# W_down of two tiles by seven block products, with the sums on GpSimd and VectorE

## The reference, cut to what matters

```python
# x: (8, 2048, 256); D = 256, INNER = 1024, 4 heads, 64 x 64 keys cut to 1024 experts
x = x + layernorm(attention(layernorm(x)))     # causal linear attention, and a memory
def ffn(hidden):
    ...                                        # scores of the keys, the best 8 of each head
    w = silu(einsum('btd,bthkd->bthk', hidden, de) * softmax(scores))
    experts_states = einsum('bthk,bthkd->btd', w, ue)
    dense = einsum('bti,di->btd', silu(einsum('btd,id->bti', hidden, W_up)), W_down)
    return dense + experts_states
x = x + layernorm(ffn(x))
```

## Time and profile before

| | us |
|---|---|
| median of 3 runs (lowest to highest) | 2823.78 (2823.51 to 2824.08) |
| the profiled execution | 2823.89 |
| its span, first to last instruction | 2822.1 |
| TensorE busy | 2796.8 |
| ACT busy | 2524.6 |
| DVE busy | 2425.9 |
| POOL busy | 2059.2 |

### The profile page before, as it was taken

One profiled execution on the slowest core, in us unless ns is written; L12 is line 12 of the kernel. 1 busy time (PEld: TensorE's weight loads), 2 busy tenths in 40 slices (PEclk: granted clock), 3 DMA queues, 4 the chain that ended last, 5 costly groups with the idle time before them and its releaser, 6 DMA issues.

```text
span 2822.1 us, 43258 instructions
## 1 busy us (share of the span) xinstructions
PE 2796.8 (99%) x11986; PEld 2179.2 (77%) x11986; DVE 2425.9 (86%) x6126; ACT 2524.6 (89%) x3619; POOL 2059.2 (73%) x2461
## 2 busy tenths in 40 slices
PE   8899999999999999999999999999999999999999
PEld 7677777777777777777777777777777777777777
DVE  6888888888888888888888888888888888888885
ACT  6888999999999899989999999999999999999997
POOL 4676777677777777777777777777777777777674
PEclk9999999999999999999999999999999999999999
DMA  4787888788878887887888888788877887887764
GB/s 131 153 172 165 173 171 173 165 176 175 170 164 176 173 167 168 174 174 165 174 173 170 165 176 175 168 164 178 174 166 169 175 173 166 173 171 167 150 152 116
DMA packets 609013, 471.27 MB, mean 167 GB/s; under 512 B 362371, under 2 KB 543492, under 8 KB 608772
## 3 DMA queue, kind: packets, MB, share of 16 engines
q0 software_dynamic: 52832, 199.77, 39.8%
q1 hardware_dynamic: 555940, 268.74, 38.3%
HBM read 137.37 MB, written 131.20 MB: 95 GB/s over the span
## 4 chain that ended last, share of the span: by engine, by line
PE 89%; POOL 5%; issue 2%; ACT 2%; DVE 2%; POOLq 0%; DVEq 0%; ACTq 0%
PE banks L763 83%; PE banks L945 4%; POOL sums L600 3%; PE banks L927 2%; POOL rstd L586 1%; POOL wexp L662 1%; ACT L1135 0%; POOL cand_best L645 0%; ACT wexp L1135 0%; DVE prob L1283 0%; DVE picked L1225 0%; POOL cdif L665 0%; DVE w_blocks L1298 0%; POOL cprob L614 0%; ACT scores L1152 0%
## 5 line engine op out<-in xcount | busy, mean ns | idle before, releaser
L600 POOL TENSOR_TENSOR sums<-scores 128x1024 f32<-128x1024 f32 x512 | 1009.2, 2063 | 80.7 <-ACT scores L1152 80.7
L586 POOL TENSOR_TENSOR rstd<-var_eps,minus_half 128x1 f32<-128x1 f32 x512 | 519.0, 1014 | 39.9 <-ACT y_sq L1064 15.5
L763 PE MATMUL banks<-deT,xn2T 128*128 128x512 f32 x1024 | 483.1, 595 | 2.6 <-DVE picked L1225 2.2
L763 PE MATMUL banks<-xn2T,wupT 128*128 128x256 f32 (+1 forms) x2272 | 464.8, 359 | 2.5 <-DVE state L1353 2.5
L763 PE MATMUL banks<-wdownT,hT 128*128 128x256 f32 x2048 | 462.8, 379 | 0.6 <-ACT hT L1011 0.6
L763 PE MATMUL banks<-ue,gT 128*128 128x256 f32 x2048 | 463.0, 379 | 0.0
L763 PEld LDWEIGHTS banks<-xn2T,wupT 128*128 128x128 f32 x2272 | 398.6, 190 | 50.9 <-DVE state L1353 3.3
L763 PEld LDWEIGHTS banks<-wdownT,hT 128*128 128x128 f32 x2048 | 389.1, 190 | 57.2 <-issue 2.8
L763 PEld LDWEIGHTS banks<-ue,gT 128*128 128x128 f32 x2048 | 389.0, 190 | 53.0 <-ACT gT L1085 0.3
L638 POOL TENSOR_TENSOR wexp<-wexp,w_last 128x1 f32<-128x1 f32 x127 | 123.8, 975 | 343.1 <-ACT z_last L1141 343.1
L763 PEld LDWEIGHTS banks<-deT,xn2T 128*128 128x128 f32 x1024 | 185.3, 191 | 135.6 <-issue 124.7
(11 more groups left out here) (173 smaller groups left out, 6552.3 us busy)
## 6 DMA issues: line engine op xcount, KB each, us to landing
wexp<-wexp POOLq DMA_DIRECT2D x127, 1024.0 KB, 9.4
wexp<-wexp POOLq DMA_DIRECT2D x127, 512.0 KB, 4.5
w_way<-w_blocks SPq DMA_DIRECT2D x127, 512.0 KB, 3.1
g_parts<-w_way SPq DMA_DIRECT2D x508, 128.0 KB, 8.0
xn_way<-xn_blocks SPq DMA_DIRECT2D x992, 32.0 KB, 1.7
x_in<-_attn_hidden_states_dram SPq DMA_DIRECT2D x128, 128.0 KB, 6.9
out_dram<-x_out SPq DMA_DIRECT2D x128, 128.0 KB, 2.8
xn1T<-xn_way SPq DMA_DIRECT2D x125, 128.0 KB, 3.5
```

The lines of the kernel that those rows point to most:

```text
L586: return nc.gpsimd.tensor_tensor(rstd[:, n, m:m + 1], var_eps[:, n, m:m + 1], minus_half[:, :], ALU.pow)
L600: return nc.gpsimd.tensor_tensor(sums[:, k, :, :], scores[:, k, 0:XIN].unsqueeze(2).broadcast_to([P, XIN, NKEYS]), scores[:, HEADS + k, :] ...
L763: last = nc.tensor.matmul(out, lhs(c), rhs(c), start=(start and c == 0), stop=(stop and c == chunks - 1))
```

## The change

**Seven products.** For tiles 12 to 121 (`SEVEN`) two tiles a and a+1 are a block of 2 x 2: rows are the tiles, columns the halves of the inner size. W_down is cut to 2 x 2 as well, into halves of the inner size and of the columns. Seven products of such blocks and sums take the place of eight. TensorE computes four in the step of the even tile and three in that of the odd one, each with 4 matmuls of 128 columns. The four sums of W_down's blocks are made once by POOL (`wdown_mix`), in four early steps. The sums of `hT` are made by POOL for every pair, in place but for `h_diff`: four of 128x512. Four blocks of results go to bank 0 and are copied to `cross` by ACT; DVE adds them up and adds bank 4 (`pair_y`). The last norm and `x_out` of these tiles come one step later.

**POOL's order.** `h_difference` (even) or `h_three` (odd) stands after the powers and ahead of `z_last`; `h_second_row` or `h_rest` waits for the weighing of head 3 and stands ahead of the next key sums of head 0. The addition of `w_last` is done by ACT, as a function with a bias, of one column.

**The first head.** `prob` of head 0 now lies over its `sums`, that of head 2 in `wexp`; the exp of head 0 waits until DVE has picked it, the next key sums of head 0 until ACT has taken the silu. DVE weighs head 0 after the pick of head 3. `x_out` is made ahead of the transposes, which now follow each other. `x_mid` has 8 places in place of 10.

```diff
-    MID_SLOTS = 10
+    MID_SLOTS = 8
+    SEVEN = (PAIRED, LATE - 4)
+    HC = IC // 2
+    DH = D // 2
+            def h_difference(a):
+                pool.wait_ge(s_hidden_1_ready, a + 1)
+                pool.wait_ge(s_hidden_0_ready, a + 1)
+                wait(pool, s_y_hidden_in_psum, a - 1)
+                nc.gpsimd.tensor_tensor(h_diff[:, :, :], h_block(a, 0), h_block(a + 1, 0), ALU.subtract).then_inc(s_h_mixed, 1)
+            def h_second_row(a):
...
+                nc.gpsimd.tensor_tensor(h_block(a + 1, 0), h_block(a + 1, 0), h_block(a + 1, 1), ALU.add).then_inc(s_h_mixed, 1)
+            def h_three(a):
...
+                nc.gpsimd.tensor_tensor(h_block(a, 0), h_block(a + 1, 0), h_block(a, 0), ALU.subtract).then_inc(s_h_mixed, 1)
+            def h_rest(a):
...
+                nc.gpsimd.tensor_tensor(h_block(a, 1), h_block(a, 1), h_block(a, 0), ALU.subtract).then_inc(s_h_mixed, 1)
@@ POOL, body
-                    pool.wait_ge(s_head_0_weights_ready, t[9] + 1)
-                    pool.wait_ge(s_last_expert_weight, t[9] + 1)
-                    nc.gpsimd.tensor_tensor(weights(t[9])[:, 0, LAST_IN:], weights(t[9])[:, 0, LAST_IN:], w_last[:, t[9] % 2:t[9] % 2 + 1], ALU.add).then_inc(s_last_expert_added, 1)
+                if seven(t[11]):
+                    pool.wait_ge(s_head_3_weighed, t[9] + 1)
+                    if t[11] % 2 == 0:
+                        h_second_row(t[11])
+                    else:
+                        h_rest(t[11] - 1)
                 if t[8] is not None:
                     pool.wait_ge(s_route_scores_ready, t[8] + 1)
+                    wait(pool, s_head_0_weights_ready, t[8])
                     key_sums(0).then_inc(s_head_0_sums_ready, 1)
@@ TensorE
+            def seven_products(t):
+                a = t // 2 * 2
+                if t == a:
...
+                    block_product(cross_ps[:, 0, :], h_block(a, 0), wdown_block(0, 0))
...
+                    block_product(cross_ps[:, 2, :], h_diff, wdown_mix[:, 2, :, :])
+                    y_made(pe, a - 1)
+                    block_product(y_bank(a)[:, 0:DH], h_block(a, 1), wdown_block(1, 0), stop=False, shared=True)
+                    block_product(y_bank(a + 1)[:, 0:DH], h_block(a + 1, 1), wdown_mix[:, 3, :, :], start=False, stop=False,
+                                  shared=True).then_inc(s_y_hidden_in_psum, 1)
+                else:
+                    pe.wait_ge(s_h_mixed, 4 * nth(a) + 4)
+                    block_product(cross_ps[:, 3, :], h_block(a + 1, 0), wdown_mix[:, 0, :, :])
+                    block_product(cross_ps[:, 1, :], h_block(a, 0), wdown_mix[:, 1, :, :])
+                    block_product(y_bank(a)[:, DH:], h_block(a, 1), wdown_block(1, 1), start=False, stop=False,
+                                  shared=True).then_inc(s_y_hidden_in_psum, 1)
@@ ACT, body
+                    nc.scalar.activation(weights(t[9], 0)[:, LAST_IN:], weights(t[9], 0)[:, LAST_IN:], ACT.Identity,
+                                         bias=w_last[:, t[9] % 2:t[9] % 2 + 1]).then_inc(s_last_expert_added, 1)
...
+                if seven(t[13]) and t[13] % 2 == 0:
+                    act.wait_ge(s_y_hidden_in_psum, t[13] + 2)
+                    wait(act, s_pair_y_ready, nth(t[13]))
+                    nc.scalar.copy(cross[:, :, :], cross_ps).then_inc(s_cross_copied, 1)
@@ DVE
+            def pair_y(a):
+                dve.wait_ge(s_cross_copied, nth(a) + 1)
+                nc.vector.tensor_tensor(cross[:, 1, :], cross[:, 0, :], cross[:, 1, :], ALU.add).then_inc(s_cross_steps, 1)
...
+                nc.vector.tensor_tensor(cross[:, 2, :], cross[:, 1, :], cross[:, 2, :], ALU.add).then_inc(s_cross_steps, 1)
...
+                nc.vector.tensor_tensor(cross[:, 1::2, :], cross[:, 1:3, :], cross[:, 3, :].unsqueeze(1).broadcast_to([P, 2, DH]),
+                                        ALU.add).then_inc(s_cross_steps, 1)
...
+                nc.vector.tensor_tensor(y_sb[:, :, 0:D], bank[4].rearrange("p (t n) -> p t n", n=D),
+                                        cross[:, :, :].rearrange("p (t k) n -> p t (k n)", t=2), ALU.add).then_inc(s_pair_y_ready, 1)
```

208 lines of the change are left out of this document (148 added, 60 removed).

## The result

| | before | after |
|---|---|---|
| median of the runs | 2823.9 us (2823.5 to 2824.1) | 2919.8 us (2916.7 to 2923.4) |
| ratio | 1 | 1.034, 95% interval 1.0322 to 1.0358 |
| the profiled execution: span | 2822.1 us | 2921.7 us |
| granted TensorE clock | 1.00 | 1.00 |

The changed kernel is 96 us slower. Slower was forecast, and by the loop that was forecast, but 57 us less of it: 2919.8 lies outside the range of 2797 to 2900.

A forecast was written before the change was run, and what follows sets the result against it. TensorE bounds the kernel before; after the change a POOL and DVE loop of 22.0 us a tile does, against 21.59. 2823.9 + 45 (110 tiles) - 6 (ends) = 2863 us; forecast 2835 to 2895 (0.60), 8-in-10 range 2797 to 2900.

The forecast's parts named there:

- What bounds the kernel before: Kernel before: TensorE's own work at full clock, 21.59 us a tile; the POOL, DVE and ACT loop closes in 20.8.
- TensorE's saving: W_down products on TensorE: 6.90 us a pair falls to 6.25, saving 0.65 a pair, 36 us over 55 pairs.
- TensorE stays the bound: Rival: POOL's second sum fits in before ACT's scores arrive, giving 2782 us; chance 0.17 for below 2808.
- The new loop: POOL's second sum waits for DVE's head 3 weighing, next head 0 key sums queue behind it; this loop becomes the bound.
- The length of the loop: Loop from head 0's key sums to the next: 21.8 us, plus 0.2 for pair_y, makes 22.0 us a tile.
- The second sum: POOL's h_second_row or h_rest, between head 3's weighing and the next head 0 key sums: 1.02 us a tile.
- The first sum and head 2's weighing: POOL's h_diff or h_three, between x_mid's power and z_last: placed where POOL has room, no cost taken.
- slower by more: Rival: every DVE addition and POOL sum collides, 22.5 us a tile, 2918 us; chance 0.08 for more than 2895.
- Head 0's weighing beside the key sums of head 2: DVE's weighing begins some 0.3 us before POOL's third key sums end and collides on SBUF: 0.2 us added.
- pair_y: DVE's four additions ahead of dens, 1.7 us a pair, fall on POOL's candidate sums: loop delayed 0.4 a pair, 0.2 a tile.
- ACT's part: ACT's changed copies and adds are hidden in its 2.3 us idle a tile: costed at nothing, 0.5 a tile if uncovered.
- The ends: Some 5 tiles at both ends, where head 0's weighing is off the way to cmask: -6 us, between 0 and 25.

The follow-up runs named there:

- e1: Changed kernel with no tile on the seven products (all tiles by eight), rest of the change kept: 2819.2 us, ratio 0.9984 to the kernel before.
- e9: Changed kernel with POOL's four hT sums and DVE's four pair_y additions cut to 8 columns, results left wrong: 2801.2 us, ratio 0.992 to the kernel before.
- e5: Changed kernel with DVE's pair_y moved from ahead of the denominators to just behind their reciprocal: 2916.4 us, ratio 1.0326 to the kernel before.
- e7: Changed kernel with POOL's first sums (h_diff, h_three) cut to 8 columns, second sums whole, results left wrong: 2884.2 us, ratio 1.021 to the kernel before.
- e10: Changed kernel with pair_y's four additions cut to 8 columns, POOL's sums whole, results left wrong: 2900.2 us, ratio 1.0271 to the kernel before.
- e3: Changed kernel with all four of POOL's hT sums cut to 8 columns, results left wrong: 2832.1 us, ratio 1.0027 to the kernel before.

## Why the prediction came out as it did

**What bounds the kernel before: right.** e1 and e9 show both ends: with 8 products and no new work TensorE is the bound, with 7 products and (nearly) no new work it is again.

**TensorE's saving: right in the rows, too large in the time.** 6.25 us a pair were forecast and stand in the trace. In e9, where it counts, the pair gains 0.49 us instead of 0.65. It changes nothing in the result, since in the changed kernel all of it turns into waiting, as forecast. The rival "TensorE stays the bound" with its 2782 us was out of reach: with all new work of the others small it is 2801.

**The new loop: right.** The second sum begins 0.08 us after head 3's weighing ends (1471.67 to 1471.75), the key sums directly behind it, TensorE waits 1.51 us for the masked scores in the step shown and 58.7 us in all, head 0's weighing takes over 1.28 us. Two signs came out otherwise: TensorE also waits 37.4 us for ACT's `mix`, which I had not forecast (e5 shows that this wait costs next to nothing), and DVE's wait before `dens` is not gone but down from 128.2 to 56.6 us. Without the collisions named below the loop closes in 21.98 us (e7) where I had 21.8.

**The length of the loop: wrong, by 0.47 us a tile.** Term by term, from 22.0 to 22.47:

- *The second sum*, forecast 1.02 us from the `ue` sums of the earlier trace rows, takes 1.27 us in the mean, and 1.23 from its start to that of the key sums. The row I took it from had the same shape, but one operand that is broadcast. The two other stretches of the loop are in e7 what I had: 10.38 us from the key sums to x_mid (1455.09 to 1465.47, forecast 10.4) and 10.29 from there to the end of head 3's weighing (1475.76, forecast 10.3). So this term (0.21 more, against 0.03 less in the others) makes 21.98 of my 21.8: 0.18 us a tile, 20 us.
- *The first sum and head 2's weighing*: nothing in the value that I took; only the end of 22.3 and the rival "slower by more" had collisions of POOL's sums. I wrote that the first sum stands "where POOL has room", and looked only at POOL; but it blocks the weighing that stands beside it on DVE, and that one is on the path. e7 gives its price, 36 us, 0.33 a tile. This is the step that failed: the rule that I had used two paragraphs further on, for head 0's weighing, I did not apply to every new instruction of POOL.
- *Head 0's weighing beside the key sums of head 2*: forecast 0.2, measured 1526 against 1279 ns, 0.25; it is part of the 10.29 us above.
- *pair_y*: forecast 0.2 a tile, measured 20 us, 0.18 a tile (e10). The Trainium skill's rule (SBUF — State Buffer, section "SBUF: two separate sides") would, as I had read it, have made 1.0 a pair of it. The trace agrees with the rule for these short additions too: the first one takes 0.49 us in the changed kernel, beside the end of the key sums, against 0.28 in e3. But the other two keep their time (292 and 425 ns in the mean, in e3 as well), and it is POOL that pays for them: its four candidate sums take 1.36 us instead of 1.02, which is the 0.36 a pair of e10.

21.98 + 0.33 + 0.18 are 22.49, against 22.47 seen. **The rival "slower by more"** (22.5 a tile, 2918 us) had nearly the right number by a partly wrong list: not every addition of DVE collides, but every first sum does, by 0.1 us or by more, as the next paragraphs show. I gave all above 2895 a chance of 0.08.

**Why the first sum costs so much.** Its price is not the same in every step. Timelines of the changed kernel, of POOL (first fence) and DVE (second fence):

```profile
1443.13 1.55 POOL L657 TENSOR_TENSOR h_diff<-hT 128x512 f32<-128x512 f32 x1
1444.36 1.66 POOL L714 TENSOR_TENSOR z_last<-cprob,rz 128x112 f32<-128x112 f32 x1
```

```profile
1443.81 2.00 DVE L1403 SCALAR_TENSOR_TENSOR wexp<-picked,rz,wexp 128x1024 f32<-128x1024 f32 x1
...
1489.48 1.37 DVE L1403 SCALAR_TENSOR_TENSOR wexp<-picked,rz,wexp 128x1024 f32<-128x1024 f32 x1
```

In the first of these steps POOL had waited for its own DMA on `wexp` (L697), so that its row is late and the weighing waits out the first sum and `z_last`. In the other it had not: the weighing waits for the end of the sum alone, and `z_last` waits for the weighing (1.34 us at 1489.74, against 437 ns in the mean of e7). Over the 109 steps from the first second sum to the last there are 73 without that wait, with 1.37 us for the weighing in the mean (e7: 1.27), and 36 with it, with 1.96 us. So by an estimate from these means some 24 of the 36 us come from the steps with a late DMA. Timeline of POOL before (first fence), and its waits after (second fence):

```profile
1430.58 1.22 POOL L662 DMA_DIRECT2D wexp<-wexp  x1
...
1442.03 0.88 POOL L619 DMA_DIRECT2D wexp<-wexp  x1
```

```profile
POOL wexp L697 <- DMA wexp<-wexp: 23.1, 38, 1.4
```

Before, POOL came to L619 11.45 us after it had issued the DMA that L619 waits for, and never had to wait; after, it comes to L697 after 10.14 us (1476.31 to 1486.45), since `cmask` is free earlier (POOL waits 0.85 us for it and not 2.04), and that DMA takes 9.4 us in the median and 11.2 at most. e1 has the same distance and 25 such waits (13.8 us), so the DMA is late by the new order and not by the seven products; it cost nothing there. e7 has 25 too, and its weighing keeps 1.27 us in the median. So the larger part of the price comes where a late DMA and a sum behind it meet. This is read from rows; no run took the DMA's wait away and left the sums whole.

**ACT's part: right**, nothing of it shows in e1. **The ends: right**, 4 us by e1, forecast 6.

**What stays open.** The steps of the changed kernel are not equal, 22.1 to 23.5 us in the middle; the DMA wait and `pair_y` account for the long ones that I looked at. No order was tried in which L697 stands later or its first DMA is issued earlier. The cause of the loss of some 6 us in the last tiles of e9 was not looked for either.

## What to carry to other kernels

- Work put on GpSimd has two prices: its own time, if something waits for it, and the time for which it blocks the DVE instruction beside it. Go through *every* added GpSimd instruction and name the DVE instruction that runs then; "GpSimd is idle here" is half of the question. Here the overlap was paid, on one side or the other, wherever that DVE instruction read two tensors from SBUF (x_out, the weighings) or was a `tensor_scalar` from SBUF to SBUF (xn).
- Before taking work from the bounding engine, write down how far behind it the second bound is, in us per round. Here it was 0.8 us a tile, the saving was worth 0.25 to 0.3, and the second loop grew by 1.7 (from 20.8 to 22.47).
- A wait may have a second use. The wait for head 3's weighing looked like a pure loss of one sum a tile, and moving it cost 162 us, since it also kept the key sums off the weighing.
- A wait that was never needed has a margin. The new order brought POOL 1.3 us nearer to its own DMA (11.45 to 10.14 us); that cost nothing by itself and much once a sum stood behind it.

## What was not expected of the hardware

- A sum of 128x512 on GpSimd took 1.23 to 1.27 us with two full operands, 1.02 with one of them broadcast along a row.
- Beside such a sum a 256-column `tensor_scalar` with one tensor operand took 1.67 us instead of 0.41, x_out 1.49 instead of 0.48; a transpose of 256 columns kept its 0.40 to 0.44. A pick of 1024 columns with an operand in PSUM kept its 1.27 to 1.28 beside the key sums.
- fp32 matmuls with 128 columns followed each other at 112 ns (3.57 us for 32), with 256 columns at 216 (3.45 us for 16): by these distances 64 short ones would take 0.24 us more than 32 long ones of the same work.
